# Gate product stored with its residual: a separate last pass folded into the output-projection tiles of an eight-core attention layer

## Chip, cores and metric

One Trainium2 chip, 8 cores, each with its own batch element and no exchange between them. The metric is device time in microseconds of the slowest core. TensorE is called PE, VectorE DVE, ScalarE ACT, GpSimd POOL and SyncE SP.

## What is computed

One layer, for x of 8 x 2048 x 4096 in fp32; a core has one of the eight:

```python
xn = layernorm(x)
s  = attn(xn, Wq, Wk, Wv, Wo)        # gated linear attention + sliding window, 32 heads of 128, then @ Wo
g  = silu(ffn(xn, W0, b0, A, B))     # xn @ W0.T + b0 + 2 * sum_l mask_l * (xn A_l.T) B_l.T / keep
return x + s * g
```

The last line is what this case is about: the product s * g in the transposed layout (features on partitions), its transpose back to tokens on partitions, and the sum with x.

## The kernel before

One long schedule is written down once in `build_walk` and replayed for each engine: every `op` or `dma` names the stream (T, V, S, SY, G for PE, DVE, ACT, SP, POOL) on which it stands, its event and the events that it waits for. Each stream runs in the order of the text, so whatever stands behind a waiting entry on the same stream waits too. DMA queues are fed by SP, ACT (transposes only, in this part) and POOL. SP's transfers use six semaphores in turn, POOL's four, ACT's two, and a transfer waits for the last one on its semaphore.

The stages: layernorm and transpose (to about 400 us); the gate g by feature tile, spilled to DRAM as `g_sp` in fp32; the V, K and Q projections, spilled; then from 3230 us the attention in 16 chunks of 128 tokens (c = 0 to 15). After each chunk from c = 4 on, eight tiles of the output projection follow (`emit_p5_jtile`), so 12 groups of eight, and after the last chunk 32 more with ts = 3. Such a tile is 128 output features (j) by 512 tokens (ts), `it = 4*j + ts`. Two tiles share a block of 256 columns of Wo, loaded by POOL as `wo` with a cast from fp32 to bf16 into one of two buffers; the load waits for the matmuls of the block before the last.

A tile before the change:

- `gld` on SP (L367): the gate tile, 128 x 512 fp32, into one of two buffers
- `p5mm` on PE (L375): 32 matmuls into the one PSUM bank `pWo`; it waits for `sg` of the tile before
- `sg` on DVE (L384): `pWo` times the gate, to bf16
- `sgt` on ACT's queue (L388): DMA transpose to tokens on partitions
- `sgsp` on SP (L395): 128 KB to `sg_sp` in DRAM, in pieces of 256 B

On SP the order is gld, sgsp, gld, sgsp. After the last tile comes the final pass: for each of the 16 blocks of 128 tokens and each half of the columns, `p6sg` on SP (L662) reads `sg_sp` back, `p6x` on POOL (L668) reads x, `p6add` on DVE (L673) adds, `p6st` on SP (L677) writes the output. Its buffers lie over those of the attention.

Of the tile, the lines that set the order:

```python
waits=[f"wo.{ts}.{b}", ...] + ([f"sg.{prev}"] if prev is not None else [])   # p5mm
waits=[f"sg.{it}"] + ([f"sgsp.{pprev}"] if pprev is not None else [])        # sgt
waits=[f"sgt.{it}"]                                                          # sgsp
```

Of the kernel before, what the change touches and what calls it, by code (L numbers as in the profile page):

```python
# [7 lines left out]
F32 = mybir.dt.float32  # L8
BF16 = mybir.dt.bfloat16
AF = mybir.ActivationFunctionType  # L10
ALU = mybir.AluOpType
# [3 lines left out]
D = 4096  # L15
# [4 lines left out]
NTT = NT // 128  # L20
# [12 lines left out]
class Walk:  # L33
# [26 lines left out]
    def op(self, stream, name, emit_fn, waits=()):  # L60
        serial = stream in ("V", "S", "G")
        sem = STREAM_SEM[stream]
        if self.mode == "collect":
            self._wait(waits)
            return
        if self.mode == "count":
            if serial:
                self.C[sem] += 1
                if name is not None:
                    self.evt[name] = (sem, self.C[sem])  # L70
            elif name is not None and name in self.waited:
                self.C[sem] += 1
                self.evt[name] = (sem, self.C[sem])
            return
        if self.stream != stream:
            return
        self._wait(waits)
        if serial and self.C[sem] > 0:
            self.eng.wait_ge(self.sems[sem], self.C[sem])
        instr = emit_fn(self.eng)  # L80
        if serial:
            self.C[sem] += 1
            instr.then_inc(self.sems[sem], 1)
        elif name is not None and name in self.waited:
            self.C[sem] += 1
            instr.then_inc(self.sems[sem], 1)
# [6 lines left out]
    def dma(self, stream, name, emit_fn, waits=()):  # L93
        if self.mode == "collect":
            self._wait(waits)
            return
        pool = DMA_POOL[stream]
        sem = pool[self.dn[stream] % len(pool)]
        self.dn[stream] += 1
        if self.mode == "count":  # L100
            self.C[sem] += 16
            self.evt[name] = (sem, self.C[sem])
            return
        if self.stream != stream:
            return
        self._wait(waits, is_dma=True)
        if self.C[sem] > 0 and self.hwm.get(sem, -1) < self.C[sem]:
            self.eng.wait_ge(self.sems[sem], self.C[sem])
            self.hwm[sem] = self.C[sem]
        instr = emit_fn(self.eng)  # L110
        self.C[sem] += 16
        instr.then_inc(self.sems[sem], 16)
# [8 lines left out]
def build_walk(w, t):  # L121
    op, dma = w.op, w.dma
# [9 lines left out]
    for i in range(NTT):  # L132
# [4 lines left out]
            lambda e, i=i, xb=xb: e.dma_start(out=xb, in_=t["x_h"][i * 128:(i + 1) * 128, :]),  # L137
            waits=[f"p1xn.{i-2}"] if i >= 2 else [])
# [3 lines left out]
           waits=[f"p1x.{i}"] + ([f"p1r.{i-2}"] if i >= 2 else []))  # L142
# [3 lines left out]
           waits=[f"p1x.{i}"] + ([f"p1xn.{i-2}"] if i >= 2 else []))  # L146
# [6 lines left out]
           waits=[f"p1sq.{i}"])  # L153
# [4 lines left out]
           waits=[f"p1r.{i}", f"p1nm.{i}"] + ([f"p1tr.{i-2}"] if i >= 2 else []))  # L158
        dma("S", f"p1tr.{i}",
            lambda e, i=i, ib=ib: e.dma_start_transpose(  # L160
                t["bigA"][:].rearrange("p (c tt) -> p c tt", c=32)[:, :, i * 128:(i + 1) * 128],
                t["xn_tm"][ib]),
            waits=[f"p1xn.{i}"])
# [4 lines left out]
                              in_=t["acat_h"][:].rearrange("(k p) m -> p k m", p=128)),  # L168
        waits=P1_END)
    dma("G", "w_bt", lambda e: e.dma_start(out=t["bt"], in_=t["bt_h"][:]), waits=P1_END)  # L170
    xn = t["bigA"][:].rearrange("p (k tt) -> p k tt", k=32)
    for ts in range(4):
        def mm_h(e, ts=ts):
# [6 lines left out]
           waits=["w_acat", f"p1tr.{NTT-1}"] + ([f"p2hev.{ts-1}"] if ts else []))  # L180
        op("S", f"p2hev.{ts}",
           lambda e, ts=ts: e.copy(t["h"][:, ts * 512:(ts + 1) * 512], pb[0][:]),
           waits=[f"p2h.{ts}"])
# [9 lines left out]
    for lt in range(128):  # L193
        j, ts = lt // 4, lt % 4
# [4 lines left out]
            waits=P1_END if lt < 2 else [f"p2tl3.{lt - 2}"])  # L199
# [60 lines left out]
    for vq in range(4):  # L260
# [4 lines left out]
            waits=[f"p2mm.{119 + 8 * vq}"] if vq < 2 else [f"p3vmm.{(vq-1)*16 - 1}"])  # L265
        for tt in range(16):
            it = vq * 16 + tt

            def mm_v(e, vq=vq, tt=tt, it=it):
# [14 lines left out]
                waits=[f"p3vev.{it}"])  # L284
    for b in range(4):
# [5 lines left out]
        for sub in range(8):  # L291
            j2, ts = sub // 4, sub % 4
            j = b * 2 + j2
# [63 lines left out]
    def emit_p5_jtile(ts, j):  # L357
        b, j2 = j // 2, j % 2
        it = j * 4 + ts
        if j2 == 0:  # L360
            emit_p5_block(ts, b)
        ei = len(p5_seq)
        prev = p5_seq[-1] if p5_seq else None
        pprev = p5_seq[-2] if len(p5_seq) >= 2 else None
        p5_seq.append(it)
        dma("SY", f"gld.{it}",
            lambda e, j=j, ts=ts, ei=ei: e.dma_start(  # L367
                out=t["gld5"][ei % 2], in_=t["g_sp"][j, :, ts * 512:(ts + 1) * 512]),
            waits=[f"p2gs.{it}"] + ([f"sg.{pprev}"] if pprev is not None else []))

        def mm_s(e, b=b, j2=j2, ts=ts):
            wb = t["wobuf"][b % 2].rearrange("p (k m) -> p k m", k=32)
            off = (4 * ts % 8) * 128
            for k in range(32):
                ii = e.matmul(t["pWo"][:], wb[:, k, j2 * 128:j2 * 128 + 128],  # L375
                              bass.AP(t["bigA"][:].tensor, k * 1024 + off,
                                      [[32 * NT, 128], [1, 512]]),
                              start=(k == 0), stop=(k == 31))
            return ii
        op("T", f"p5mm.{it}", mm_s,  # L380
           waits=[f"wo.{ts}.{b}", f"oev.{4*ts+3}.{KVH-1}"] +
                 ([f"sg.{prev}"] if prev is not None else []))
        op("V", f"sg.{it}",
           lambda e, it=it, ei=ei: e.tensor_tensor(t["sgv5"][ei % 2], t["pWo"][:],  # L384
                                                   t["gld5"][ei % 2], ALU.mult),
           waits=[f"p5mm.{it}", f"gld.{it}"] + ([f"sgt.{pprev}"] if pprev is not None else []))
        dma("S", f"sgt.{it}",
            lambda e, it=it, ei=ei: e.dma_start_transpose(  # L388
                t["sgt5"][ei % 2].rearrange("p (r q) -> p r q", r=4),
                t["sgv5"][ei % 2]),  # L390
            waits=[f"sg.{it}"] + ([f"sgsp.{pprev}"] if pprev is not None else []))
        dst = bass.AP(t["sg_sp"].tensor, ts * 512 * D + j * 128,
                      [[D, 128], [128 * D, 4], [1, 128]])
        dma("SY", f"sgsp.{it}",
            lambda e, dst=dst, it=it, ei=ei: e.dma_start(  # L395
                out=dst, in_=t["sgt5"][ei % 2].rearrange("p (r q) -> p r q", r=4)),
            waits=[f"sgt.{it}"])

    def emit_pass2(c, gg, cr):
        hs = slice(gg * 128, (gg + 1) * 128)  # L400
# [255 lines left out]
    P4_END = [f"p4odone.{NCH-1}", f"sadd.{NCH-1}.{KVH-1}", f"sbf.{NCH-1}",  # L656
              f"p4kdone.{NCH-1}", f"khTev.{NCH-1}", f"sq.{NCH-1}.{KVH-1}", f"qt1.{NCH-1}.{KVH-1}"]

    for i2 in range(2 * NTT):
        i, hf = i2 // 2, i2 % 2  # L660
        dma("SY", f"p6sg.{i2}",
            lambda e, i=i, hf=hf, i2=i2: e.dma_start(  # L662
                out=t["sgh"][i2 % 2],
                in_=t["sg_sp"][i * 128:(i + 1) * 128, hf * 2048:(hf + 1) * 2048]),
            waits=[f"sgsp.{j*4+3}" for j in range(26, 32)] + [f"gld.{j*4+3}" for j in range(29, 32)]
                  + ([f"p6add.{i2-2}"] if i2 >= 2 else []))
        dma("G", f"p6x.{i2}",
            lambda e, i=i, hf=hf, i2=i2: e.dma_start(  # L668
                out=t["xf"][i2 % 2],
                in_=t["x_h"][i * 128:(i + 1) * 128, hf * 2048:(hf + 1) * 2048]),  # L670
            waits=([f"p6add.{i2-2}"] if i2 >= 2 else [f"sg.{127}"]))
        op("V", f"p6add.{i2}",
           lambda e, i2=i2: e.tensor_tensor(t["of"][i2 % 2], t["xf"][i2 % 2],  # L673
                                            t["sgh"][i2 % 2], ALU.add),
           waits=[f"p6sg.{i2}", f"p6x.{i2}"] + ([f"p6st.{i2-2}"] if i2 >= 2 else [f"sgsp.{127}"]))
        dma("SY", f"p6st.{i2}",
            lambda e, i=i, hf=hf, i2=i2: e.dma_start(  # L677
                out=t["out_h"][i * 128:(i + 1) * 128, hf * 2048:(hf + 1) * 2048],
                in_=t["of"][i2 % 2]),
            waits=[f"p6add.{i2}"])  # L680
    op("SY", "fin", lambda e: e.nop(), waits=[f"p6st.{2*NTT-1}"])


def build_nc():
# [31 lines left out]
    with ctx:  # L716
# [15 lines left out]
        def V_(off, n, dt=BF16):  # L732
            ap = pool[:, off:off + n]
            if dt == F32:
                ap = ap.bitcast(F32)
            return ap
# [58 lines left out]
        def BV(off, n, dt=BF16):  # L795
            ap = t["bigA"][:][:, off:off + n]
            if dt == F32:
                ap = ap.bitcast(F32)
            return ap
# [3 lines left out]
        t["sgt5"] = [BV(52224, 512), BV(52736, 512)]  # L803
        t["qt18"] = [BV(53248 + 512 * i, 512) for i in range(8)]
        t["sqa8"] = [BV(57344 + 512 * i, 512) for i in range(8)]
        t["xf"] = [V_(0, 4096, F32), V_(4096, 4096, F32)]
        t["of"] = [V_(8192, 4096, F32), V_(12288, 4096, F32)]
        t["sgh"] = [V_(16384, 2048), V_(18432, 2048)]
# [134 lines left out]
```

## Time and profile before

| | us |
|---|---|
| timed runs before | 6978.06 and 7414.96, median 7196.51 |
| profiled execution | 6993.7 |
| its span, slowest core (core 6) | 6992.2 |
| spans of all eight cores | 6938.7 to 6992.2 |
| mean granted clock of TensorE | 0.810 to 0.816 |

The whole page and the trace are of the profiled execution, on core 6. The page gives each engine's busy time, then the span in 40 slices of 175 us each with the busy share in tenths, the queues, and the chain of work that ended last, followed back from the last instruction. The trace was asked for that chain in order of time (start, duration, what it was: an engine and line, or a transfer), for stretches of the span (a row has start:end and length, busy us and number of instructions of PE, PEld, DVE, ACT and POOL, then granted clock, DMA share and GB/s), for who waited for whom, and for the queues of a stretch (packets, MB, share of 16 engines). A DMA engine's time is what a queue's share says: share times 16 times the stretch.

### The profile page before, as it was taken

What the parts mean: (1) busy time and instruction counts of PE and PEld (TensorE: products, weight loads), DVE (VectorE), ACT (ScalarE), POOL (GpSimd) and SP (SyncE); (2) the same over time, 40 slices, a digit from 0 to 9 for tenths busy, and PEclk for the clock granted to TensorE, in tenths of its full rate; (3) what the DMA queues carried; (4) which work ended last, traced back from release to release, by engine and by line L of the source; (5) the groups of instructions that cost most, each with busy time, mean ns of one, the idle gap of its engine ahead of it and who ended that gap; (6) DMA issues with size and microseconds to landing.
All of it is one profiled execution on the core that took longest, in us unless ns stands there. A gap on an engine that the chain in (4) does not pass through costs nothing.

```text
span 6992.2 us, 53281 instructions; the slowest of 8 cores (6938.7 to 6992.2 us)
## 1 busy us (share of the span) xinstructions
PE 4233.2 (61%) x18137; PEld 1767.7 (25%) x18464; DVE 1369.1 (20%) x2248; ACT 1169.4 (17%) x1662; POOL 291.7 (4%) x272
## 2 busy tenths in 40 slices
PE   0067777777899999996355544465445654466600
PEld 0023333323485444442011111121111211122200
DVE  2212222222200000002442221122221222210022
ACT  4410000000010000002442221122221222200000
POOL 0000000000000000000000000000000000000000
PEclk9999999989999999997557676776677766688855
DMA  4454444434433334432004335543355433568877
GB/s 141 141 86 95 95 92 92 92 89 89 96 56 56 55 55 62 61 55 45 19 12 61 51 61 78 75 64 49 57 81 75 64 55 53 78 94 124 114 229 255
DMA packets 825323, 577.52 MB, mean 83 GB/s; under 512 B 306272, under 2 KB 757088, under 8 KB 814688
## 3 DMA queue, kind: packets, MB, share of 16 engines
q0 software_dynamic: 454944, 320.88, 29.4%
q1 hardware_dynamic: 234432, 219.65, 11.8%
q10 hardware_dynamic: 135680, 33.57, 3.1%
q8 instruction: 150, 2.46, 0.2%
q14 instruction: 117, 0.96, 0.1%
HBM read 651.61 MB, written 109.05 MB: 109 GB/s over the span
## 4 chain that ended last, share of the span: by engine, by line
PE 46%; DMA 26%; ACT 11%; DVE 8%; issue 5%; ACTq 3%; SPq 1%; DVEq 0%; another core or an unknown queue 0%; POOLq 0%; POOL 0%
PE pb L326 13%; PE pb L210 12%; DMA bigA<-g_sp 8%; DMA bigA<-bigA 7%; PE pWo L375 6%; DMA pool<-maskt 3%; PE pb L272 3%; DMA pool<-sg_sp 3%; PE pb L299 3%; ACTq L160 2%; PE pb L239 2%; DMA pool<-q_sp 2%; DVE bigA L384 1%; ACT pool L245 1%; DVE pool L673 1%
## 5 line engine op out<-in xcount | busy, mean ns | idle before, releaser
L375 PE MATMUL pWo<-bigA 128*128 128x512 bf16 x4015 | 1017.3, 414 | 589.5 <-DVE bigA L384 585.0
L210 PE MATMUL pb<-bigA,pool 128*128 128x512 bf16 x4020 | 929.6, 387 | 138.7 <-ACT pool L245 133.3
L326 PE MATMUL pb<-bigA,pool 128*128 128x512 bf16 x4014 | 879.9, 379 | 4.3
L375 PEld LDWEIGHTS pWo<-bigA 128*128 128x128 bf16 x4096 | 420.4, 105 | 1181.3 <-issue 796.6
L227 DVE TENSOR_TENSOR pool<-pb,pool 128x512 bf16<-128x512 f32 x512 | 354.3, 692 | 1166.6 <-PE pb L239 694.5
L210 PEld LDWEIGHTS pb<-bigA,pool 128*128 128x128 bf16 x4096 | 399.0, 99 | 674.8 <-issue 238.3
L326 PEld LDWEIGHTS pb<-bigA,pool 128*128 128x128 bf16 x4096 | 400.8, 98 | 483.3
L384 DVE TENSOR_TENSOR bigA<-pWo,bigA 128x512 bf16<-128x512 f32 x128 | 88.6, 692 | 1480.7 <-DMA bigA<-g_sp 1115.3
L465 DVE TENSOR_TENSOR_SCAN pool<-onesf_sb,pool 128x128 f32<-128x128 f32 x128 | 54.4, 425 | 1573.8 <-ACT pool L463 1561.9
L245 ACT ACTIVATE pool<-pb,b_sb 128x512 f32<-128x512 f32 x128 | 87.9, 687 | 1351.0 <-PE pb L239 1350.9
L176 PE MATMUL pb<-bigA,pool 128*128 128x512 bf16 x126 | 30.7, 403 | 408.7 <-DMA pool<-acat 406.0
L545 PE MATMUL pb<-pool,twos_sb 128*128 128x512 bf16 x121 | 70.8, 585 | 340.1 <-ACT pool L542 340.1
L352 POOL DMA_DIRECT2D bigA<-wo x64 | 107.3, 1676 | 3269.2 <-PE pWo L375 3269.2
L482 PE MATMUL pb<-pool,ones_sb 128*128 128x512 bf16 x16 | 9.4, 585 | 384.6 <-ACT pool L479 384.6
L272 PE MATMUL pb<-pool,bigA 128*128 128x256 bf16 x2048 | 226.2, 274 | 2.2 <-DMA pool<-wv 2.2
L461 ACT ACT_TABLE_LOAD x16 | 20.5, 1283 | 1237.6 <-DMA pool<-v_sp 672.1
L299 PE MATMUL pb<-bigA,pool 128*128 128x512 bf16 x1003 | 219.9, 379 | 1.1
L333 ACT CAST pool<-pb 128x512 bf16<-128x512 f32 x128 | 75.0, 586 | 809.0 <-PE pb L326 809.0
L272 PEld LDWEIGHTS pb<-pool,bigA 128*128 128x128 bf16 x2048 | 201.6, 98 | 27.1 <-issue 2.7
L219 PE MATMUL pb<-pool 16*128 16x512 bf16 x512 | 53.6, 408 | 202.5 <-DVE pool L227 202.5
L610 PE MATMUL pb<-pool,twos_sb 128*128 128x512 bf16 x124 | 62.3, 503 | 143.0 <-ACT pool L606 134.5
L239 PE MATMUL pb<-pool,id_sb 128*128 128x512 bf16 x486 | 138.4, 408 | 7.9 <-issue 4.5
(111 smaller groups left out, 3246.1 us busy)
## 6 DMA issues: line engine op xcount, KB each, us to landing
bigA<-wo POOLq DMA_DIRECT2D x64, 2048.0 KB, 18.5
pool<-maskt POOLq DMA_DIRECT2D x128, 512.0 KB, 4.5
pool<-x SPq DMA_DIRECT2D x16, 2048.0 KB, 8.3
pool<-w0t POOLq DMA_DIRECT2D x16, 2048.0 KB, 16.7
g_sp<-pool SPq DMA_DIRECT2D x128, 256.0 KB, 2.6
pool<-wq POOLq DMA_DIRECT2D x16, 2048.0 KB, 16.6
bigA<-g_sp SPq DMA_DIRECT2D x128, 256.0 KB, 5.9
pool<-x POOLq DMA_DIRECT2D x32, 1024.0 KB, 9.2
```

The costliest lines, as they stand in the source:

```text
L160: lambda e, i=i, ib=ib: e.dma_start_transpose(t["bigA"][:].rearrange("p (c tt) -> p c tt", c=32)[:, :, i * 128:(i + 1) * 128], t["xn_tm"][ ...
L210: ii = e.matmul(pb[bk][:], wb[:, k, j2 * 128:j2 * 128 + 128], xn[:, k, ts * 512:(ts + 1) * 512], start=(k == 0), stop=False)
L227: lambda e, l=l, ts=ts, it=it: e.tensor_tensor(t["tl"][l], pb[l][:], t["mbig"][it % 2].rearrange("p (l4 tt) -> p l4 tt", l4=4)[:, l, :], A ...
L239: ii = e.matmul(pb[bk][:], t["id128_sb"][:], t["tl"][l], start=False, stop=(l == 3))
L245: lambda e, it=it, j=j, bk=bk: e.activation(t["gv"][it % 2], pb[bk][:], AF.Silu, bias=t["b0_sb"][:, j:j + 1]),
L272: ii = e.matmul(pb[4 + it % 2][:, 0:256], xn[:, k, tt * 128:(tt + 1) * 128], wb[:, k, :], start=(k == 0), stop=(k == 31))
L299: ii = e.matmul(pb[4 + it % 2][:], wb[:, k, j2 * 128:j2 * 128 + 128], xn[:, k, ts * 512:(ts + 1) * 512], start=(k == 0), stop=(k == 31))
L326: ii = e.matmul(pb[4 + it % 2][:], wb[:, k, j2 * 128:j2 * 128 + 128], xn[:, k, ts * 512:(ts + 1) * 512], start=(k == 0), stop=(k == 31))
L333: lambda e, it=it: e.copy(t["ev"][it % 4], pb[4 + it % 2][:]),
L352: lambda e, src=src, b=b: e.dma_start(out=t["wobuf"][b % 2], in_=src),
L375: ii = e.matmul(t["pWo"][:], wb[:, k, j2 * 128:j2 * 128 + 128], bass.AP(t["bigA"][:].tensor, k * 1024 + off, [[32 * NT, 128], [1, 512]]), ...
L384: lambda e, it=it, ei=ei: e.tensor_tensor(t["sgv5"][ei % 2], t["pWo"][:], t["gld5"][ei % 2], ALU.mult),
```

## The change

The final pass is removed. Each output-projection tile now reads its own piece of x and writes its own piece of the output. A new `xld` on POOL loads x for the tile (128 tokens x 4 x 128 columns, 256 KB in pieces of 512 B); it stands behind `wo` of a new block and waits for `xadd` two tiles before. A new `scop` on ACT copies `pWo` to SBUF in fp32 (`sgf5`), and `p5mm` of the next tile waits for `scop` instead of `sg`. `sg` reads that copy. After the transpose a new `xadd` on DVE adds x and writes fp32 over `sgf5`, and `outst` on SP writes it to the output in pieces of 512 B, 256 KB, where `sgsp` stood. On SP the order is now gld, outst, gld, outst; on DVE sg, xadd, sg, xadd; on ACT scop, sgt, scop, sgt. `sgf5` and `xld5` are four new buffers at the end of `bigA`.

```diff
+        dma("G", f"xld.{it}",
+            lambda e, j=j, ts=ts, ei=ei: e.dma_start(
+                out=t["xld5"][ei % 2],
+                in_=bass.AP(t["x_h"].tensor, ts * 512 * D + j * 128,
+                            [[D, 128], [128 * D, 4], [1, 128]])),
+            waits=[f"xadd.{pprev}"] if pprev is not None else [])
...
         op("T", f"p5mm.{it}", mm_s,
            waits=[f"wo.{ts}.{b}", f"oev.{4*ts+3}.{KVH-1}"] +
-                 ([f"sg.{prev}"] if prev is not None else []))
+                 ([f"scop.{prev}"] if prev is not None else []))
+        op("S", f"scop.{it}",
+           lambda e, ei=ei: e.copy(t["sgf5"][ei % 2], t["pWo"][:]),
+           waits=[f"p5mm.{it}"] + ([f"sg.{pprev}", f"outst.{pprev}"] if pprev is not None else []))
         op("V", f"sg.{it}",
-           lambda e, it=it, ei=ei: e.tensor_tensor(t["sgv5"][ei % 2], t["pWo"][:],
+           lambda e, it=it, ei=ei: e.tensor_tensor(t["sgv5"][ei % 2], t["sgf5"][ei % 2],
                                                    t["gld5"][ei % 2], ALU.mult),
-           waits=[f"p5mm.{it}", f"gld.{it}"] + ([f"sgt.{pprev}"] if pprev is not None else []))
+           waits=[f"scop.{it}", f"gld.{it}"] + ([f"sgt.{pprev}"] if pprev is not None else []))
...
-            waits=[f"sg.{it}"] + ([f"sgsp.{pprev}"] if pprev is not None else []))
-        dst = bass.AP(t["sg_sp"].tensor, ts * 512 * D + j * 128,
-                      [[D, 128], [128 * D, 4], [1, 128]])
-        dma("SY", f"sgsp.{it}",
-            lambda e, dst=dst, it=it, ei=ei: e.dma_start(
-                out=dst, in_=t["sgt5"][ei % 2].rearrange("p (r q) -> p r q", r=4)),
-            waits=[f"sgt.{it}"])
+            waits=[f"sg.{it}"] + ([f"xadd.{pprev}"] if pprev is not None else []))
+        op("V", f"xadd.{it}",
+           lambda e, ei=ei: e.tensor_tensor(t["sgf5"][ei % 2].bitcast(BF16).bitcast(F32),
+                                            t["xld5"][ei % 2], t["sgt5"][ei % 2], ALU.add),
+           waits=[f"sgt.{it}", f"xld.{it}"] + ([f"outst.{pprev}"] if pprev is not None else []))
+        dma("SY", f"outst.{it}",
+            lambda e, j=j, ts=ts, ei=ei: e.dma_start(
+                out=bass.AP(t["out_h"].tensor, ts * 512 * D + j * 128,
+                            [[D, 128], [128 * D, 4], [1, 128]]),
+                in_=t["sgf5"][ei % 2].bitcast(BF16).bitcast(F32)),
+            waits=[f"xadd.{it}"])
...
-    for i2 in range(2 * NTT):
...
-    op("SY", "fin", lambda e: e.nop(), waits=[f"p6st.{2*NTT-1}"])
+    fin_w = [f"outst.{j*4+3}" for j in range(26, 32)] + [f"gld.{j*4+3}" for j in range(29, 32)]
+    op("SY", "fin", lambda e: e.nop(), waits=fin_w)
...
+        t["sgf5"] = [BV(61440, 1024, F32), BV(62464, 1024, F32)]
+        t["xld5"] = [BV(63488, 1024, F32), BV(64512, 1024, F32)]
```

## Rows read from the trace of the kernel before

**Rows 1.** The page's 40 slices of the span, busy tenths: PE and DMA

```profile
PE   0067777777899999996355544465445654466600
DMA  4454444434433334432004335543355433568877
```

**Rows 2.** The page's chain that ended last, by engine and by line

```profile
PE 46%; DMA 26%; ACT 11%; DVE 8%; issue 5%; ACTq 3%; SPq 1%; DVEq 0%; another core or an unknown queue 0%; POOLq 0%; POOL 0%
PE pb L326 13%; PE pb L210 12%; DMA bigA<-g_sp 8%; DMA bigA<-bigA 7%; PE pWo L375 6%; DMA pool<-maskt 3%; PE pb L272 3%; DMA pool<-sg_sp 3%; PE pb L299 3%; ACTq L160 2%; PE pb L239 2%; DMA pool<-q_sp 2%; DVE bigA L384 1%; ACT pool L245 1%; DVE pool L673 1%
```

**Rows 3.** Stretches: a group of eight tiles, a chunk, last tiles, final pass

```profile
5924.60:6029.20 104.60, 65.49 (x252) 26.61 (x254) 7.76 (x12) 1.60 (x4) 6.70 (x4) 0.83 0.75 104
6029.20:6139.50 110.30, 45.87 (x123) 11.08 (x126) 45.92 (x88) 47.30 (x73) 0.00 (x0) 0.59 0.16 30
6206.00:6652.00 446.00, 274.16 (x1079) 112.70 (x1099) 23.52 (x34) 0.00 (x0) 26.81 (x16) 0.83 0.83 116
6664.90:6992.20 327.30, 0.00 (x0) 0.00 (x0) 73.36 (x32) 0.00 (x0) 15.86 (x30) 0.50 0.75 250
```

**Rows 4.** Chain in order of time, among the last tiles: start us, us, what

```profile
6467.77 4.52 DMA bigA<-g_sp
6473.40 9.58 DMA bigA<-bigA
6483.62 7.52 DMA bigA<-g_sp
6492.22 9.49 PE pWo L375 x32
6502.88 4.10 DMA bigA<-bigA
```

**Rows 5.** Timeline of POOL in the same stretch: start us, us, what

```profile
6472.47 1.68 POOL L352 DMA_DIRECT2D bigA<-wo  x1 [22.28 <-PE pWo L375]
6502.41 1.67 POOL L352 DMA_DIRECT2D bigA<-wo  x1 [28.26 <-PE pWo L375]
```

**Rows 6.** Line L352, the wo loads, whole span: time from issue to landing

```profile
DMA to landing us min/median/max: 16.2/18.5/26.3
```

**Rows 7.** Chain in order of time: last tiles and start of the final pass

```profile
6643.66 2.49 DMA bigA<-bigA
...
6658.67 5.99 DMA sg_sp<-bigA
6664.88 5.38 DMA pool<-sg_sp
```

**Rows 8.** Waits, 3750 to 6652 us: total us, times, longest

```profile
DVE bigA L384 <- DMA bigA<-g_sp: 1106.8, 81, 20.9
...
DVE bigA L384 <- PE pWo L375: 365.4, 46, 10.5
```

**Rows 9.** Groups of instructions, whole span: count, busy us, mean ns, idle before

```profile
L384 DVE TENSOR_TENSOR bigA<-pWo,bigA 128x512 bf16<-128x512 f32 x128 | 88.6, 692 | 1480.7 <-DMA bigA<-g_sp 1115.3 <-PE pWo L375 365.4
L549 ACT ACTIVATE pool<-pb 128x512 f32<-128x512 f32 x128 | 76.4, 597 | 113.5 <-PE pb L545 105.0 <-remote 6.2 <-PE pb L556 2.3
L673 DVE TENSOR_TENSOR pool<-pool 128x2048 f32<-128x2048 f32 x32 | 73.4, 2292 | 261.8 <-DMA pool<-sg_sp 261.8
```

**Rows 10.** Queues in 2450 to 3090 us, Q projection, 256 B stores on q1

```profile
q0 software_dynamic: 49344, 25.17, 29.7%
q1 hardware_dynamic: 49104, 12.20, 8.5%
```

**Rows 11.** Queues in 1970 to 2150 us, V projection, 512 B stores on q1

```profile
DMA packets 21143, 10.21 MB, mean 57 GB/s; under 512 B 2384, under 2 KB 21128, under 8 KB 21128
q1 hardware_dynamic: 8208, 3.41, 7.2%
```

**Rows 12.** Queues in 500 to 1900 us, gate stage, masks and w0t

```profile
q0 software_dynamic: 79258, 94.98, 34.1%
pool<-maskt POOLq DMA_DIRECT2D x121, 512.0 KB, 4.5
```

**Rows 13.** Chain in order of time, start of a chunk behind a group

```profile
5814.23 8.36 DMA pool<-k_sp
```

More of the change, by code:

```diff
@@ L657, in build_walk @@
               f"p4kdone.{NCH-1}", f"khTev.{NCH-1}", f"sq.{NCH-1}.{KVH-1}", f"qt1.{NCH-1}.{KVH-1}"]
-    for i2 in range(2 * NTT):
[L660 to L680, printed above, removed]
-    op("SY", "fin", lambda e: e.nop(), waits=[f"p6st.{2*NTT-1}"])
+    fin_w = [f"outst.{j*4+3}" for j in range(26, 32)] + [f"gld.{j*4+3}" for j in range(29, 32)]
+    op("SY", "fin", lambda e: e.nop(), waits=fin_w)
 def build_nc():
```

## The prediction

> **What bounds the kernel now.** I read the page's engine table and slices first [rows 1]. No engine is the bound of the second half: from slice 22 on PE is busy mostly four to six tenths, and in the last two slices it does nothing while DMA is at seven. The chain that ended last [rows 2] names the transfers instead: the gate load bigA<-g_sp 8%, the transpose bigA<-bigA 7%, the reload pool<-sg_sp 3%. The table of stretches [rows 3] shows three kinds of stage: about 105 us for each of the 12 groups of eight output tiles, about 110 us for each attention chunk between them, then 32 output tiles in a row, and from 6664.9 us the final pass of 327.3 us (32 steps, 0.75 DMA share, no matmul). In 6206 to 6652 the table has 34 DVE instructions, one L384 for each tile: 446/34 = 13.1 us a tile.
>
> What makes 13.1 us is in the chain through three tiles [rows 4] and POOL's order there [rows 5]. SP issues gld of tile n+1 (L367) directly behind the store sgsp of tile n (L395), and that store waits for the transpose. So the loop is: sg (0.7 us), transpose, sgsp, gate load, sg. The loads of wo set the size of its steps. POOL issues one of 2 MB (written) every second tile, when the matmuls of the odd tile end; it is in flight 18.5 us at the median [rows 6]. A transpose that starts 0.9 us behind one takes 9.58 us, one that starts 0.5 us behind takes 4.10 [rows 4, 5], one far from any 2.49 [rows 7]; a gate load takes 7.52 us beside a wo load and 4.52 away from it [rows 4]. About every fourth step is set by the matmuls (9.49 us) because p5mm waits for sg of the tile before. DVE waited for gate loads 1107 us and for the matmuls 365 [rows 8].
>
> **The change, part by part.** The sum is made against the profiled execution, 6993.7 us (span 6992.2). The two runs of the table are 6978 and 7415; the sum stands beside the first, and their median of 7196.5 is no base for it.
>
> *Removed: the final pass.* From the first reload at 6664.88 [rows 7] to the end of the span: -327.3 us. The last sgsp took 5.99 us to land ahead of it, and the last outst now takes its place: nothing more.
>
> *Added on the path: xadd.* The transpose is now followed by a DVE add and then by outst, behind which gld of the next tile still stands on SP. The add of 2048 columns takes 2.292 us [rows 9], 512 columns a quarter, so 0.6 with its start. From the gate load's landing (6483.62+7.52 = 6491.14) to the next matmul (6492.22) pass 1.08 us [rows 4], of which sg is 0.69 [rows 9]; I give 0.25 of the rest to DVE's start behind a landing. That is +0.85 a tile. SP's issue of outst is taken as that of sgsp, which is inside the 0.64 us from the transpose's landing (6473.40+9.58 = 6482.98) to the gate load's start (6483.62 [rows 4]). sg reads SBUF instead of PSUM: 0.6 for 0.69, -0.1.
>
> *Moved: the matmuls off the loop.* scop empties pWo in about the 0.6 us of ACT's L549, which reads the same PSUM shape [rows 9], and p5mm of the next tile waits for that, no longer for sg and its gate load. ACT's queue keeps scop behind the transpose of the tile before, so PE gets one tile ahead. Matmuls plus scop are 9.49+0.75, about 10.3 us, below any period below, so they leave the path. The gain is the slack that the PE-bound steps had, about 1 us in every fourth: -0.3 a tile. The first tile of each group ends with scop+sg instead of sg: +0.7 x 12 = 8 us.
>
> *Moved: the x loads, behind which the wo loads now stand on POOL.* xld of tile n+2 waits for xadd of tile n, and wo for the next block is queued behind it. So wo starts not at the end of the odd tile's matmuls but after its xadd, 5 to 10 us later. It is still early enough. Counting from the odd xadd: xld's issue about 0.6, wo issued at 0.7, landed by 21 (18.5 now [rows 6], plus 2 for the new traffic); the matmuls that need it take to 31, and the gate of that tile lands at about 35. The cover is 4 us; the slack of a whole four-tile cycle is about 5. What it does change is which step meets wo.
>
> *Price of the new transfers.* Per tile 256 KB of x in 512 pieces of 512 B, and 256 KB of output in 512 pieces, for 128 KB in 512 pieces of 256 B. Stores of 256 B: 8.5% of 16 engines x 640 us over 49104 packets is 17.7 ns [rows 10]. In 1970 to 2150, 7.2% x 16 x 180 = 207 us, less 2384 x 17.7 ns, over the other 5824 packets, nearly all of 512 B, is 28 ns [rows 11]. So outst costs 0.9 us of all 16 engines for 0.57, +0.35. For the x load the nearest is the mask, also 512 pieces on POOL's queue but 1 KB each: 34.1% x 16 x 1400 = 7638 us, less 16 weight loads of 4096 packets at 61.6 ns (29.7% x 16 x 640 / 49344 [rows 10]), over its 121 masks, is 1.86 us of 16 engines [rows 12]. Half the bytes: 0.9 if bytes count, 1.9 if pieces do. Together +1.25 to +2.25 us of DMA per tile, on a share of 0.83, or 10.9 us, of 13.1 [rows 3].
>
> Here the 17.7 against 28 ns bears on a rule. The Trainium skill (DMA: Bandwidth & Descriptors, Specifications) says that transfers below 512 B are not at line rate because the engine reads and rewrites. If that halved the rate of the old stores, outst would cost nothing beside sgsp and the sum would be some 40 us lower (0.35 x 115 from 6805 is 6765, inside the forecast case below). By the row, 256 B takes two thirds of the time of 512 B, so most of the difference stands.
>
> *The new pair of tiles,* from the end of the odd tile's xadd (0): gate load issued at 0.6 (the 0.64 us above). It goes out before wo's data come in force, but behind the larger store and beside xld: 6.0 us, between the 4.5 and 7.5 of rows. Then 0.25, sg 0.6, 0.2, and a transpose fully beside wo: 9.6, as the worst row, because it starts 7 us in. Then 0.25, xadd 0.6: 18.1 us. Second half: 0.6, gate load 5.5 (4.5 and a share of the new traffic), 0.25+0.6+0.2, transpose outside wo 2.5, 0.25+0.6: 10.5. A pair takes 28.6 us for 26.2, +1.2 a tile. Within groups and at the end there are 12 x 7 + 31 = 115 such steps: +138 us. The step from a group's last tile into the next chunk loses the early wo (transpose 4.1 to 2.5, the k load from its 8.36 us [rows 13] to less) and gains xadd: between -3 and +1 each; with the +8 above I take zero for both. Sum: 6993.7 - 327.3 + 138 = 6804, rounded to 6805 us.
>
> Bounds of the step: with no loss to the new traffic only +0.85-0.1-0.3, about +0.5 a tile (6724 us). With the even gate load at 8.3 and the odd at 6.5, +2.9 a tile (7000 us). I stand nearer the low side because at an odd xadd the gate load and wo start together, where rows show a transfer that starts before wo's data get through in 4 us [rows 4, 5].
>
> **The rivals.**
>
> (1) *Cheap contention*, near +0.5 a tile or less: 6724 us. For it: PE leaves the path, and the gate load escapes wo. Against it: every new byte is released at the moment when the gate load is issued.
>
> (2) *Dear contention*: the even gate load still takes 8 to 9 us as [rows 4] show beside wo. +1.7 to +2.9 a tile: 6860 to 7000 us, within 2%. For it: share 0.83 already. The same page of the Trainium skill (Queues, rings and completion order) has each engine take packets from its queues in turn. By that, outst directly ahead of the gate load on SP's queue delays it in full, and wo only in part, as assumed.
>
> (3) *The DMA engines become the bound*, the slower side: with every new piece at the 61.6 ns of a wq piece [rows 10] x costs 512 x 61.6 / 16 = 2.0 us and outst 2.0 for 0.57, so a tile needs 10.9+3.4 = 14.3 us of all engines; if the share stays at 0.83 the tile takes 17.2 us, and +4.1 x 128 = 525 gives 7191 us. It decides from 16.75 us a tile, (7134-6666)/128 = 3.65 more than now. Against it: the prices without contention give 12.2 to 13.2 us of engine time.
>
> (4) *wo arrives late*: POOL's wait for xadd pushes it past the matmuls. A four-tile cycle is then wo 0.7+21, matmuls 9.5, scop and sg 1.5, transpose 9.6, xadd, gate 5.5+1.5, transpose and xadd 3.5+0.85, near 55 us against 57.2. From a wo landing of 24 us it binds; at its present maximum of 26.3 [rows 6] a tile is +0.6: 6880 us.
>
> (5) *It saves nothing*, because the x load isn't there when xadd comes: against it, each is released two tiles (28 us) before its use, and a wo load of eight times the pieces lands in 18.5 [rows 6]. It would give back what it saves: 6994 us.
>
> **How the numbers follow.** Forecast case, steps of +0.7 to +1.6: 0.47, at 6805 us. Rival 1: 0.15. Rivals 2 and 4: 0.28. Rival 3: 0.07, rival 5: 0.03. About 2% is what a measurement of this kernel can tell from no change; that is 6854 below and 7134 above. The forecast case and rival 1 lie below 6854: faster 0.62. Rivals 2, 4 and 5 lie within: 0.31. Slower 0.07. Range 6720 to 6960 us, down to rival 1's and up into rival 2, leaving out its dear end and rival 3.
>
> **What would show it.** The final pass gone: no pool<-sg_sp, and matmuls almost to the end. xadd at 0.6 us. The tile loop in the last 32 tiles at 14.3 us for 13.1, with DVE waiting for the gate load or for the transpose and hardly for PE. Transposes behind odd tiles at 2.5 us, behind even ones near 9. wo issued after xadd. The forecast is wrong if PE waits for wo, if gate loads behind odd tiles take 8 us, if the DMA share passes 0.93, or if the tile is below 13.3 us.

## The result and the profile after

The kernel after takes 0.950 of the time before, 95% interval 0.946 to 0.953. Its timed runs begin at 6607.6 us, those of before at 6976.8. In some executions of every eight-core program the cores of one die run at a lower granted clock and the time is several per cent longer; all comparisons here leave those out, and where few runs remain they name the shortest ones. The forecast was 6805 us, with a range from 6720: the direction was right, the time some 165 us too long, below the range.

The profiled execution after has a span of 6696.0 us on core 0. On that core the gate stage, far ahead of the change, took some 84 us longer than on core 6 (last store of `g_sp` at 1985.6 against 1902.1 us; first sg at 3849 against 3763), so I read core 6, whose span is 6610.7 us, against core 6 of before (6992.2, first sg at 3761). The difference is 381 us, all of it behind the first sg.

Stretches of the kernel after, core 6 (start:end, length, busy us of PE, PEld, DVE, ACT, POOL with counts, granted clock, DMA share, GB/s): a chunk, the last tiles, and what follows the last sg.

```profile
5965.00:6083.00 118.00, 54.66 (x123) 12.11 (x126) 47.31 (x90) 47.30 (x73) 2.44 (x2) 0.50 0.22 43
6160.00:6604.00 444.00, 269.70 (x1046) 110.47 (x1065) 46.18 (x67) 19.89 (x34) 52.03 (x49) 0.82 0.97 145
6604.00:6611.00 7.00, 0.00 (x0) 0.00 (x0) 0.92 (x2) 0.00 (x0) 0.00 (x0) 0.56 0.22 56
```

Where [rows 3] had a pass of 327.3 us with no matmul there are 7 us now. 34 ACT instructions (one scop a tile) in 444 us are 13.1 us a tile, in a stretch whose DMA share rose from 0.83 to 0.97. Such a count is rough at its edges: by the starts of sg, core 6 makes a last tile in 12.9 us before and 13.2 after.

The chain that ended last, in order of time, through two of the last tiles of after, core 6:

```profile
6399.76 2.44 DMA bigA<-bigA
6403.80 4.10 DMA bigA<-g_sp
6408.89 8.00 DMA bigA<-bigA
6417.18 0.70 DVE bigA L402
6418.50 7.47 DMA bigA<-g_sp
6426.95 2.46 DMA bigA<-bigA
6431.02 4.44 DMA bigA<-g_sp
```

POOL's timeline there, and DVE's xadd (L402) and sg (L393):

```profile
6403.80 0.75 POOL L371 DMA_DIRECT2D bigA<-x  x1 [9.39 <-DVE bigA L402]
6404.61 1.69 POOL L352 DMA_DIRECT2D bigA<-wo  x1
```

```profile
6402.49 0.69 DVE L402 TENSOR_TENSOR bigA<-bigA 128x512 f32<-128x512 f32 x1 [2.87 <-DMA bigA<-bigA]
6408.06 0.69 DVE L393 TENSOR_TENSOR bigA<-bigA 128x512 bf16<-128x512 f32 x1 [4.88 <-DMA bigA<-g_sp]
6417.18 0.69 DVE L402 TENSOR_TENSOR bigA<-bigA 128x512 f32<-128x512 f32 x1 [8.43 <-DMA bigA<-bigA]
```

Against [rows 4, 5]: the wo load is issued at 6404.61, 1.4 us behind the end of an xadd and not at the end of the matmuls. The transpose behind the odd tile is now 2.44 us and the one behind the even tile 8.00. Averaged over the last tiles of all eight cores they take 2.5 and 8.1 us, where the kernel before had 6.0 behind the odd and 3.4 behind the even tile. The matmuls (9.49 in [rows 4]) are gone from the chain here. From one odd xadd to the next pass 27.2 us.

The other place is the way into a chunk. The chain of after, core 6, at the end of a group, to set against [rows 13]:

```profile
5967.79 2.47 DMA bigA<-bigA
5971.86 3.00 DMA pool<-k_sp
5974.98 1.28 ACT L474
```

The k load lands in 3.00 us where it took 8.36. Over the whole span its median is 3.0 us for 8.0, and that of the gate load 4.9 for 5.9.

The waits of after, core 6, 3750 to 6611 us (who waited for whom: us in total, times, longest):

```profile
ACT bigA L390 <- PE pWo L381: 1372.3, 124, 23.6
DVE bigA L393 <- DMA bigA<-g_sp: 701.7, 116, 8.3
DVE bigA L402 <- DMA bigA<-bigA: 699.6, 128, 11.9
...
PE pWo L381 <- DMA bigA<-wo: 436.0, 40, 15.8
```

sg waits for its gate load almost always ([rows 8] had 81 such waits and 46 for the matmuls). PE does wait for wo, 40 times.

To compare kernels I took from each profile the starts of all 128 sg, averaged over the eight cores:

| kernel | step in a group | step in the last 32 | last tile of a group to first of the next | first sg to last sg | last sg to end |
|---|---|---|---|---|---|
| before | 12.7 | 13.0 | 126.8 | 2878 | 345 |
| before, without the pass | 13.0 | 13.1 | 127.0 | 2910 | 19 |
| before, wo later | 12.4 | 12.9 | 119.0 | 2763 | 361 |
| before, wo later, without the pass | 12.3 | 12.9 | 119.0 | 2752 | 19 |
| after | 12.9 | 13.4 | 121.2 | 2841 | 7 |
| after, two further profiles | 13.1 | 13.5 | 121.0 | 2863, 2860 | 7, 8 |
| after, PE waits for sg | 13.6 | 14.4 | 120.6 | 2929 | 7 |
| after, wo early | 13.5 | 13.5 | 127.1 | 2967 | 7 |
| after, no x loads | 14.6 | 13.5 | 121.0 | 2987 | 7 |
| after, no x loads, wo late | 12.7 | 13.2 | 120.6 | 2810 | 7 |
| gate load ahead | 11.4 | 13.1 | 126.9 | 2775 | 8 |
| gate and k load ahead | 11.3 | 13.2 | 118.0 | 2678 | 7 |
| gate and k load ahead, wo early | 10.9 | 11.7 | 115.8 | 2567 | 7 |

Two profiles of the same tile code differ by up to 1% here (2878 and 2910). What the table says: the removed pass is worth some 338 us (345 becomes 7); the steps grew by 0.2 to 0.6 us against the kernel before, and by at most 0.4 against its twin without the pass, where 1.2 was forecast; and each way into a chunk got 5.6 to 6 us shorter where nothing was forecast.

### The profile page after: what moved, and what is told of

Its sections match the earlier page's. It is cut to its first block, busy times and chain, and to the rows that moved or that the text cites. A ratio compares the mean times of both kernels' runs of the same rounds, so it can differ in the third digit from the quotient of the medians.

```text
span 6696.0 us, 54047 instructions; the slowest of 8 cores (6570.3 to 6696.0 us)
## 1 busy us (share of the span) xinstructions
PE 4284.5 (64%) x18137; PEld 1778.0 (27%) x18464; DVE 1384.0 (21%) x2344; ACT 1244.1 (19%) x1790; POOL 372.6 (6%) x368
## 3 DMA queue, kind: packets, MB, share of 16 engines
q1 hardware_dynamic: 225216, 186.09, 10.9%
## 4 chain that ended last, share of the span: by engine, by line
PE 45%; DMA 25%; ACT 12%; DVE 9%; issue 5%; ACTq 3%; SPq 1%; DVEq 1%; another core or an unknown queue 0%; POOLq 0%; POOL 0%
PE pb L210 13%; PE pb L326 13%; DMA bigA<-bigA 9%; DMA bigA<-g_sp 9%; DMA pool<-maskt 4%; PE pb L272 3%; PE pb L299 3%; ACTq L160 2%; PE pb L239 2%; DMA pool<-q_sp 1%; PE pWo L381 1%; DVE bigA L393 1%; DVE bigA L402 1%; ACT pool L245 1%; ACT pool L619 1%
## 5 line engine op out<-in xcount | busy, mean ns | idle before, releaser
L381 PE MATMUL pWo<-bigA 128*128 128x512 bf16 x4015 | 982.6, 404 | 510.2 <-DMA bigA<-wo 434.3
L210 PE MATMUL pb<-bigA,pool 128*128 128x512 bf16 x4020 | 1004.6, 410 | 139.8 <-ACT pool L245 133.3
L326 PE MATMUL pb<-bigA,pool 128*128 128x512 bf16 x4014 | 879.9, 379 | 4.3
L210 PEld LDWEIGHTS pb<-bigA,pool 128*128 128x128 bf16 x4096 | 416.0, 104 | 733.3 <-issue 467.5
L326 PEld LDWEIGHTS pb<-bigA,pool 128*128 128x128 bf16 x4096 | 400.8, 98 | 483.3
L390 ACT COPY bigA<-pWo 128x512 f32<-128x512 f32 x128 | 74.9, 585 | 1400.5 <-PE pWo L381 1325.6
L176 PE MATMUL pb<-bigA,pool 128*128 128x512 bf16 x126 | 34.3, 438 | 408.3 <-DMA pool<-acat 405.5
L558 PE MATMUL pb<-pool,twos_sb 128*128 128x512 bf16 x121 | 70.8, 585 | 340.2 <-ACT pool L555 340.2
L371 POOL DMA_DIRECT2D bigA<-x x128 | 96.6, 755 | 3147.0 <-DVE bigA L402 3096.0
L393 DVE TENSOR_TENSOR bigA<-bigA 128x512 bf16<-128x512 f32 x128 | 88.6, 692 | 762.6 <-DMA bigA<-g_sp 708.2
L402 DVE TENSOR_TENSOR bigA<-bigA 128x512 f32<-128x512 f32 x128 | 88.6, 692 | 682.1 <-DMA bigA<-bigA 682.1
L299 PE MATMUL pb<-bigA,pool 128*128 128x512 bf16 x1003 | 219.9, 379 | 1.1
L198 POOL DMA_DIRECT2D pool<-maskt x128 | 95.9, 750 | 1081.9 <-DVE pool L227 998.5
```

The source lines that it names most:

```text
L210: ii = e.matmul(pb[bk][:], wb[:, k, j2 * 128:j2 * 128 + 128], xn[:, k, ts * 512:(ts + 1) * 512], start=(k == 0), stop=False)
L299: ii = e.matmul(pb[4 + it % 2][:], wb[:, k, j2 * 128:j2 * 128 + 128], xn[:, k, ts * 512:(ts + 1) * 512], start=(k == 0), stop=(k == 31))
L326: ii = e.matmul(pb[4 + it % 2][:], wb[:, k, j2 * 128:j2 * 128 + 128], xn[:, k, ts * 512:(ts + 1) * 512], start=(k == 0), stop=(k == 31))
L371: lambda e, j=j, ts=ts, ei=ei: e.dma_start(out=t["xld5"][ei % 2], in_=bass.AP(t["x_h"].tensor, ts * 512 * D + j * 128, [[D, 128], [128 * D ...
L402: lambda e, ei=ei: e.tensor_tensor(t["sgf5"][ei % 2].bitcast(BF16).bitcast(F32), t["xld5"][ei % 2], t["sgt5"][ei % 2], ALU.add),
```

## Experiments

The theory after this comparison: the x load that stands ahead of wo on POOL delays the wo load, and that delay is a gain of its own, at the chunk starts above all. Rivals: the gain comes from the matmuls being taken off the loop, or the new work simply costs nothing.

### PE coupled again

```diff
-                 ([f"scop.{prev}"] if prev is not None else []))
+                 ([f"scop.{prev}", f"sg.{prev}"] if prev is not None else []))
```

> The kernel after, with the matmuls of a tile waiting for sg of the tile before, as they did before the change, beside scop. Theory: taking the matmuls off the loop only saved the slack of the steps that they set, so with the wait back the short steps (10.4 us behind an odd tile) grow by 0.3 to 1 us and the whole by 20 to 60 us over the kernel after (about 6640 becomes 6660 to 6700). Rival: PE running a tile ahead is what kept the loop near 13.2 us a tile in spite of xadd; then every tile grows by 1 us or more and the whole by 130 us or more (6770 and up).

Measured: 0.959 of before (0.948 to 0.970), two shortest runs 6725 and 6732 us; on that chip the shortest of before was 7028, so the kernel after would be at about 6675. That is 50 to 67 us slower by time and 66 to 88 by the table, at the upper end of the theory's 20 to 60 or above it. The interval overlaps that of the kernel after (0.946 to 0.953), so the finding rests on the steps. The waits of its slowest core (1) show the coupling:

```profile
PE pWo L381 <- DVE bigA L393: 550.8, 108, 13.6
DVE bigA L393 <- DMA bigA<-g_sp: 481.2, 79, 9.5
```

Both kinds of step grew (last tiles 14.4 for 13.4 to 13.5, tiles in a group 13.6 for 12.9 to 13.1). Taking the matmuls off the loop is worth 0.5 to 1.0 us a tile, more than the 0.3 of slack that I gave it.

### wo early again

```diff
-        if j2 == 0:
+        if j2 == 0 and not p5_seq:
             emit_p5_block(ts, b)
+        if j2 == 1:
+            if b < 15:
+                emit_p5_block(ts, b + 1)
+            elif ts < 3:
+                emit_p5_block(ts + 1, 0)
```

> The kernel after, with the load of the next block of Wo ahead of the odd tile's x load in POOL's order, so that it is issued at the end of the odd tile's matmuls again and not behind an xadd. Theory: the later wo load is what freed the gate load behind an odd tile and the k load at the start of a chunk; with it early the step from a group's last tile to the next chunk grows by about 5 us (11 x 5 = 55) and the gate load behind the odd tile goes from 5 us toward 8: slower than the kernel after by 60 to 150 us. Rival: the place of the wo load doesn't matter and the gain at the chunk's start has another cause: within 20 us of the kernel after.

Measured: 0.962 (0.956 to 0.968), shortest 6762 us, some 87 us slower than the kernel after by the ratios. The way into a chunk is back at 127.1 us. The chain at a chunk's start, slowest core:

```profile
6081.02 4.24 DMA bigA<-g_sp
6086.24 8.46 DMA bigA<-bigA
6096.31 4.33 DMA pool<-k_sp
```

The size is as the theory had it but the place only in part: here it is the last tile's transpose (8.46 us, 2.47 in the kernel after) that meets wo, and the k load suffers little (median 4.0 us). POOL's timeline on the same core shows why:

```profile
5800.24 0.75 POOL L376 DMA_DIRECT2D bigA<-x  x1 [12.72 <-DVE bigA L407]
5800.98 1.71 POOL L352 DMA_DIRECT2D bigA<-wo  x1
```

The expectation says that the edit brings wo back to the end of the odd tile's matmuls; it doesn't. PE runs a tile ahead, so these matmuls are over by then, and what holds wo is the x load in front of it, which here waits for the xadd of an even tile (L407). In the kernel after that is the xadd of an odd tile. So wo goes one tile earlier, and what is exchanged is the transpose that it meets: over all eight cores those behind odd tiles take 8.5 us and those behind even tiles 2.5, for 2.5 and 7.3 in the kernel after. The group's last tile is an odd one, so its transpose pays. The gate loads behind odd tiles grew from 4.9 to 6.0 us on average and did not go to 8, though some on this core's chain took 6 to 10.

### Only the later wo, in the kernel before

```diff
+        wdep = wdep + [w_.replace("p5mm.", "sgt.") for w_ in wdep if w_.startswith("p5mm.")]
         dma("G", f"wo.{ts}.{b}",
```

> The kernel before, with one more wait: the load of a block of Wo also waits for the transpose of the tile whose matmuls it waits for. Nothing else is changed; the final pass stays. Theory: the transpose behind an odd tile then runs outside the wo load (6.5 us becomes 3), the k load at the chunk's start too (from landing 8 to 10 us to 4 or 5), so 11 x 5 us there and perhaps 0.3 us a tile: 6990 becomes 6900 to 6935. Rival: no gain from the place of wo alone, 6975 to 7010.

Measured: 0.980 (0.975 to 0.986), shortest 6888 and 6891 us beside 7028: 2% off the kernel before by one more wait. That is 140 us, more than the 55 to 90 expected. The way into a chunk fell from 126.8 to 119.0, and the chain of its slowest core at a chunk's start reads like that of the kernel after:

```profile
5933.02 3.61 DMA bigA<-g_sp
5937.74 2.45 DMA bigA<-bigA
5940.78 2.90 DMA pool<-k_sp
```

This is the run that shows the term missing from the prediction, without anything else of the change. It also shows something about the DMA share. Its last tiles, core 6:

```profile
6120.00:6550.00 430.00, 274.30 (x1054) 112.19 (x1077) 23.53 (x34) 0.00 (x0) 26.82 (x16) 0.84 0.93 119
```

[rows 3] had a share of 0.83 at 116 GB/s there. The share rose to 0.93 with no new transfer and nearly the same rate.

### No x loads, and the slip in it

```diff
-        dma("G", f"xld.{it}",
+        if ei < 2:
+          dma("G", f"xld.{it}",
```

> The kernel after, with x loaded for the first two tiles only and these two buffers added to every later tile: it leaves out 126 of the 128 loads of x, and its output lacks the right x. Theory: the x loads cost little on the path, 0 to 0.3 us a tile, so 0 to 35 us less than the kernel after. Rival, the price assumed in the prediction: x loads stretch the gate load behind them by 0.7 us a tile or more, so 80 us or more less.

Measured: 0.961 (0.955 to 0.966), shortest 6752 us, slower than the kernel after although it moves less. Both expectations failed, through my own edit: with the x load went what held wo back on POOL. It now goes out 0.7 us behind the matmuls that it waits for, and these run ahead of the loop, so wo is earlier still than in the wo-early kernel. The loss isn't in the same place either: the way into a chunk stays at 121.0 us, and it is the steps in a group that grew, to 14.6 us for 12.9. The next run puts the wait back.

```diff
+        wdep = wdep + [w_.replace("p5mm.", "xadd.") for w_ in wdep if w_.startswith("p5mm.")]
         dma("G", f"wo.{ts}.{b}",
```

> The kernel after without 126 of its 128 x loads (its output lacks the right x), and with the load of a block of Wo waiting for the xadd of the tile whose matmuls it waits for, as the x load ahead of it on POOL makes it wait in the kernel after. In the earlier run without x loads that wait had gone with them, so wo came early. Theory: the place of wo is what cost there; here the time is 0 to 35 us less than the kernel after, the whole price of the x traffic. Rival, the prediction's price of x: 80 us or more less.

> The kernel after, unchanged, beside the next three on one chip. 0.945 to 0.955 of the kernel before; it is what the other runs of this call are compared with.

Measured on one chip: 6600 and 6602 us without x loads, 6657 and 6669 for the kernel after (before: 7016). So x costs about 60 us, or 0.45 us a tile; by the table 31 to 53. That lies between the theory's 35 and the rival's 80, nearer the theory by the profiles and in the middle by time.

### The pass alone

```diff
-    for i2 in range(2 * NTT):
+    for i2 in range(1):
```

> The kernel before with only the first of the 32 steps of the final pass: it leaves out the rest, so most of its output isn't written. Theory: the pass is worth what its stretch shows, 31 steps of 10.2 us, 317 us less than the kernel before; the kernel after is then 10 to 50 us faster than this one, because its shorter chunk starts (11 x 5.6) outweigh its longer tiles. Rival: the pass cost more than its stretch, and the kernel after is slower than this one.

Measured on the chip of the last two: 6707 and 6712 us, 309 less than the shortest before (7016), 317 expected. The kernel after is 50 us faster than this one. Some 12 us of that are the step of the pass which this run keeps (19 us behind the last sg for 7), so everything else in the change together is a gain of about 38, where the forecast had a loss of 138.

The next has both edits in the kernel before:

```diff
+        wdep = wdep + [w_.replace("p5mm.", "sgt.") for w_ in wdep if w_.startswith("p5mm.")]
         dma("G", f"wo.{ts}.{b}",
...
-    for i2 in range(2 * NTT):
+    for i2 in range(1):
```

> The kernel before with the load of a block of Wo waiting for the transpose too, and with only the first of the 32 steps of the final pass (most of its output isn't written). It has the later wo load and no pass, but none of xadd, x loads, wider stores and matmuls ahead. Theory: the later wo load gives 110 to 150 us and the added work costs 70 to 110 in the kernel after, so this one is faster than the kernel after by 50 to 110 us (0.933 to 0.942 of the kernel before). Rival: the added work is free beside the loop, and this one is within 30 us of the kernel after.

> The kernel after, unchanged, to compare the other three of this call with on one chip: 0.945 to 0.955 of the kernel before.

Measured: 6551 and 6558 us, beside 6657 for the kernel after and 7020 for the kernel before. So the ledger, from shortest runs (chips of 7016 and 7020 for before): pass removed -309; later wo, 6707 to 6551, -156; what the change adds, 6551 to 6657, +106. The sum is -359, as 7016 to 6657. The first and the last term each lack 12 us, for the step of the pass that both runs keep: the whole pass is near -321 and what the change adds near +118. That holds x (+57, from the runs above) and the gain of the matmuls ahead (-50 to -65); the rest, 110 to 125, is what xadd and the wider store cost on the loop, 0.9 to 1.0 us a tile. The terms come from three chips, though the kernel after took 6657 us on two of them, and each rests on one to three timed runs.

### Taking the gate load out of the loop

```diff
+        if ei + 1 < 128:
+            emit_gld(ei + 1)
         dma("SY", f"outst.{it}",
```

> The kernel after, with the gate load of the next tile ahead of the output store on SP, so that it no longer waits for the transpose and xadd of this tile. Theory: the loop of 13.2 us a tile is the chain transpose, xadd, gate load; with the gate load out of it the next bound is the wo cycle (about 0.8+1.7+18.5 us, matmuls 9.5, scop and sg 1.5, transpose beside wo 8.5, and the odd tile's 5) near 11.5 to 12.5 us a tile, so 80 to 200 us less than the kernel after. Rival: the DMA engines, at 0.8 to 0.9 busy, are what holds the loop; then within 30 us of the kernel after.

Measured: 6569 and 6574 us, 88 less than the kernel after on the same chip, in the theory's range. A third run took 6648; it is the one profiled, and two of its cores reach their first sg some 75 to 100 us late, ahead of the change. The DMA engines, at 0.97 in the kernel after, were no bound. The waits of its slowest core (1), 4000 to 6500 us:

```profile
DVE bigA L414 <- DMA bigA<-bigA: 859.6, 108, 14.0
PE pWo L393 <- DMA bigA<-wo: 336.6, 31, 22.4
DVE bigA L405 <- ACT bigA L402: 318.3, 68, 15.6
```

sg (L405) now waits for scop and hardly for its gate. But steps in the last tiles fell only from 13.4 to 13.1, and the last transpose of a group meets wo again (126.9): the load of wo, which waits for xadd, is next in line.

```diff
+            if c + 1 < NCH:
+                emit_kv(c + 1)
```

> The kernel after, with the next tile's gate load ahead of the output store on SP, and the loads of K and V of the next chunk ahead of the group of eight tiles instead of behind it. Theory: the k load's 5 us and the 10 us in which it waits for the last transpose and xadd leave the way into each of 11 chunks, 11 x 8 to 15 us on top of the 85 us of the gate load: 0.92 to 0.93 of the kernel before. Rival: the chunk starts late for another cause (ACT behind the last transpose's issue), then no more than the gate load alone gave.

Here `emit_kv` issues the loads of K and V of the next chunk ahead of the group of tiles. Measured: 6466 us, a single timed run, 191 less than the kernel after beside it (6657), 0.921 of the shortest before. The way into a chunk is 118.0 us for 126.9 in the run above: the k load is off it.

The last one adds to it the edit of POOL's order shown under "wo early again".

> As the one before, and the wo load ahead of the odd tile's x load on POOL, so issued at the end of the odd tile's matmuls. With the gate load out of the loop the matmuls waited for wo (about 30 times on a core, up to 22 us in between). Theory: wo is now the bound, so here early is better, though in the kernel after it was worse: 30 to 100 us less than the run before. Rival: the transposes suffer from an early wo as they did, and it is no faster.

Measured: 6354, 6354 and 6369 us, 0.9025 of before (0.894 to 0.911), 300 us less than the kernel after on the same chip. The step in the last tiles is 11.7 us. The same place of wo, one tile earlier, that cost 87 us in the kernel after gains 112 here, just above the 30 to 100 expected, since it is now the wo load that sets the loop. The waits of its slowest core (5), 3760 to 6300 us, have no wait of sg for a gate load among the longest:

```profile
DVE bigA L419 <- DMA bigA<-bigA: 1055.8, 122, 14.3
ACT bigA L407 <- PE pWo L398: 772.7, 78, 16.7
...
ACT bigA L407 <- DMA out<-bigA: 380.2, 37, 14.2
```

The DMA share of its last tiles, core 5, is above 1:

```profile
5900.00:6340.00 440.00, 299.45 (x1190) 122.49 (x1188) 51.25 (x74) 21.65 (x37) 56.76 (x55) 0.86 1.23 164
```

## Why the prediction missed the size

Two terms carry the 165 us. The pair of tiles was put 85 to 105 us too dear, and the way into a chunk, put at nothing, was a gain of 62.

- **The pass, -327.3.** Right: 345 us from the last sg to the end became 7 on the average of the cores, and the run without the pass gave -309 in time with one of its 32 steps kept.
- **"between -3 and +1 each; with the +8 above I take zero for both."** Here the mechanism was mispriced and then dropped from the sum. The way into a chunk got 5.6 us shorter (126.8 to 121.2) although xadd adds about 1 to it: the transpose of a group's last tile no longer meets wo (5.8 us became 2.5 on the average of the cores), and the k load behind it takes 3.6 us for 8.3. I had both rows, [rows 13] among them, and named both effects, then priced them at 3 us together. 11 x 5.6 = 62 us.
- **The pair of tiles, +1.2 a tile, +138.** The mechanism was as told: which step meets wo was exchanged, matmuls left the chain. The sizes were off. In the pair shown, gate load behind the odd tile 4.10 us for the 6.0 put in (it does go out ahead of wo's data: wo is issued 0.8 us behind it), the transpose beside wo 8.00 for 9.6, against that the second gate load 7.47 for 5.5. That pair is not a typical one: the means over the last tiles of all cores are 5.2, 8.1 and 5.6 us, and 2.5 for the second transpose. A pair takes 26.9 us for 25.9 before. So +0.5 to +0.6 a tile there and +0.2 to +0.5 in groups, +30 to +55 us in all instead of +138 (0 to +25 against the kernel without the pass, so the spread of profiles is as large as the term). I took the worst row for the transpose under wo and then compared the result with an average step of before, in which the transpose behind the odd tile had 5.9 us on average: a worst case set against a mean.
- **xadd, +0.85 a tile.** Its duration is 0.69 us and not 0.6, and sg from SBUF stays at 0.69. From the landing of a transpose to the next gate load pass 1.61 us now (6408.89 + 8.00 to 6418.50) and 0.64 before, so xadd puts +0.97 on the path. The ledger leaves 0.9 to 1.0 a tile for it and the store.
- **The gate load behind a larger store.** Rival 2 took its delay from the Trainium skill (DMA: Bandwidth & Descriptors, Queues, rings and completion order). In the rows shown it doesn't appear: 4.10 us with outst ahead, 4.52 with sgsp in [rows 4]. In the means over all cores it does. With wo late in both, a gate load behind another tile takes 4.3 to 4.5 us in a group and 4.7 to 4.8 in the last tiles without the change's transfers, 4.8 and 5.2 with outst but no x, and 5.1 to 5.3 and 5.4 to 5.6 in the kernel after. So the store and x lengthen it by some 0.3 to 0.4 us each, not by the full length of a transfer. The transposes that still take 8 us beside wo fit the taking of turns between queues; no run here tells it from another way of sharing.
- **Matmuls off the loop, -0.3.** Worth 0.5 to 1.0 a tile, as the run with PE coupled again showed. It hid in the pair sum, which had the matmuls off the chain.
- **New traffic.** The queues of the last tiles have 0.97 for 0.83. At 13.1 us a tile that is 1.8 us of all engines more, and it looks like a hit for the 1.25 to 2.25 worked out, but it isn't one. The kernel before with only the later wo has 0.93 there with no new transfer, which is 0.9 us a tile more by the same sum (0.93 x 430/34 = 11.8 for 10.9). And a share passes 1: 1.23 above. So packets of one engine overlap in this count, and share times time can grow without a byte more; it is not the work of the engines, as the text ahead of the prediction and the prices from [rows 10] to [rows 12] took it. What x cost on the path is 0.25 to 0.45 us a tile.
- **Rivals.** Rival 2 is out: gate loads behind odd tiles take 4.8 to 4.9 us in groups and 5.2 to 5.4 in the last tiles, not 8 to 9. Rival 3 (DMA as the bound) is out: at a share of 0.97 the loop kept its pace, and with the gate load out of it it ran faster still. Rival 4 happened in part, PE waited for wo 40 times, and cost nothing, since PE runs a tile ahead of a loop that others set. Rival 5 is out, since sg and xadd wait for gate loads and transposes, not for x. Rival 1 was the nearest, and even it had no gain at the chunks.
- **"if the DMA share passes 0.93, or if the tile is below 13.3 us."** These were signs of a wrong forecast. Both came true, 0.97 and 13.1 to 13.2 on core 6 (13.4 on the average of the cores), and so did a third sign, that PE waits for wo. Of the three only the tile's time told of an error in the sum; the other two cost nothing.

What stays open: no run measured xadd and the wider store apart in time, and by how much a profile's tile loop varies from one execution to the next (1% in the two of the tile code before) limits every term under 30 us. Several comparisons rest on one or two timed runs.

## What to carry to other kernels

A dependency added to a bulk load is not only a risk of starting it late; it decides what the load runs beside. Where a small transfer on the critical chain is issued at the same event as a large prefetch, let the small one go first, by ordering or one more wait, as long as the prefetch still has cover; one such wait took 2% off here. When costing a rearranged loop, price old and new with the same kind of row, mean with mean. And once the chain changes (the gate load out of it), look at the order again: the place of wo that lost 87 us became the one that won 112.

## What the runs showed that I had not expected

The DMA engines' share is a poor sign of a bound: from 0.83 to 0.97 the median gate load got shorter, 5.9 to 4.9 us, because it met the bulk load less often (behind odd tiles 8.0 us became 4.9, behind even ones 4.8 became 5.4, as means of all cores), and the fastest kernel here has the highest share, 1.23. A DVE add or product of 128x512 in fp32 took 0.69 us whether its operand was in PSUM or SBUF, where a quarter of the 2.292 us for 2048 columns is 0.57. The two lengths give 1.04 ns a column and 0.16 us fixed.
